# Depthwise 3x3 convolution split over three engines: GpSimd takes the last addition, VectorE gets a fifth tap for the first image, transposes move between the halves of a convolution

## The reference

```python
x = x + conv_block(_ln_c(x))      # x: (32, 128, 32, 32)
# conv_block(v): avg and max of each image and channel -> 9 taps per (image, channel) by softmax;
#   depthwise 3x3 of v with these taps, + bias, + v
t = tokens(x)                     # 32 * 1024 tokens of 128 channels
t = t + moe(_ln_t(t))             # gate to 8 experts, top 2, softmax of the 2;
                                  # per expert gelu(t @ W1 + b1) @ W2 + b2, H = 512
```

## Time and profile before

| | |
|---|---|
| median of 3 runs (lowest, highest) | 1531.86 us (1531.59, 1535.68) |
| the profiled execution | 1534.89 us, span 1532.4 us |
| busy share of the span: TensorE / VectorE / ScalarE / GpSimd | 95% / 85% / 72% / 63% |
| steps of phase A | about 31 us each |

### The profile page before, as it was taken

How to read it: one execution, slowest core, us unless ns; L and a number is a source line. 1 busy time by engine, 2 the same in 40 slices (tenths; PEclk the granted TensorE clock), 3 DMA queues, 4 the chain that set the end, 5 groups by cost and what they waited for, 6 DMA issues and landing times.

```text
span 1532.4 us, 45755 instructions
## 1 busy us (share of the span) xinstructions
PE 1453.9 (95%) x12204; PEld 1114.6 (73%) x12205; DVE 1308.8 (85%) x2676; ACT 1096.7 (72%) x2514; POOL 961.6 (63%) x1069
## 2 busy tenths in 40 slices
PE   5999999999999867999999999999999999999996
PEld 2345454555545433999999999999999999999995
DVE  2468888888888984999999999999989999999995
ACT  5477777878777523777777777777777777777773
POOL 2004455545555674777777777777777777777773
PEclk8899999999999955999999999999999999999998
DMA  4211212121222127111111232223232322222222
GB/s 141 74 38 57 70 63 81 63 75 58 77 69 64 40 71 151 41 47 40 44 43 57 66 93 86 92 86 93 85 94 83 92 86 91 84 86 78 78 75 109
DMA packets 85647, 115.77 MB, mean 76 GB/s; under 512 B 17613, under 2 KB 69865, under 8 KB 85590
## 3 DMA queue, kind: packets, MB, share of 16 engines
q1 hardware_dynamic: 64886, 76.83, 17.0%
q0 software_dynamic: 18112, 34.27, 7.0%
q10 hardware_dynamic: 2592, 4.00, 0.9%
HBM read 60.08 MB, written 58.48 MB: 77 GB/s over the span
## 4 chain that ended last, share of the span: by engine, by line
POOL 38%; PE 24%; issue 23%; DVE 6%; ACT 4%; DMA 2%; POOLq 2%; SPq 1%; ACTq 0%; DVEq 0%
PE psV L902 14%; POOL token_out L542 14%; POOL xn L530 14%; POOL yt L537 9%; PE psA L840 4%; PE psV L849 3%; DVE x L1235 2%; POOL rows_by_pair L512 1%; ACT cv L628 1%; PE psT L884 1%; ACT diag L618 1%; PE psG L886 1%; DMA stage<-in_L_ffn_W_dram 1%; ACT lnv L601 1%; POOLq L542 1%
## 5 line engine op out<-in xcount | busy, mean ns | idle before, releaser
L1495 DVE TENSOR_TENSOR gl<-g,gh 128x512 f16<-128x512 f32 x620 | 489.1, 828 | 71.1 <-ACT gh L777 61.2
L512 POOL DMA_INDIRECT rows_by_pair<-rows,idx x256 | 263.6, 1030 | 318.7 <-issue 196.1
L542 POOL DMA_INDIRECT token_out<-yt,rt x310 | 338.7, 1093 | 184.7 <-POOL yt L537 133.6
L902 PE MATMUL psV<-lp,diag 128*128 128x512 f32 x576 | 274.4, 613 | 20.5 <-ACT cv L628 20.5
L777 ACT ACTIVATE gh<-g 128x512 f16<-128x512 f32 x465 | 274.5, 624 | 16.8
L770 ACT ACTIVATE g<-psT 128x512 f32<-128x512 f32 x310 | 182.2, 597 | 101.3 <-PE psT L1057 74.4
L770 ACT ACTIVATE g<-psV 128x512 f32<-128x512 f32 x310 | 184.8, 597 | 90.1 <-PE psV L1057 62.0
L530 POOL TENSOR_SCALAR xn<-rt 128x128 f32<-128x128 f32 x310 | 221.5, 721 | 14.0 <-DMA rt<-rows_by_pair 10.1
L1078 PE MATMUL psR<-wall,gh 128*128 x1240 | 221.3, 273 | 0.4 <-DVE ya L1512 0.4
L1078 PE MATMUL psG<-wall,gh 128*128 x1240 | 221.3, 273 | 0.0
L902 PEld LDWEIGHTS psV<-lp,diag 128*128 128x128 f32 x576 | 106.2, 193 | 150.9 <-issue 108.2
(11 more groups left out here) (231 smaller groups left out, 2950.2 us busy)
## 6 DMA issues: line engine op xcount, KB each, us to landing
rt<-rows_by_pair SPq DMA_DIRECT2D x155, 133.0 KB, 2.1
xb<-in_x_dram SPq DMA_DIRECT2D x32, 512.0 KB, 3.5
yq<-token_out SPq DMA_DIRECT2D x112, 128.0 KB, 2.4
out_dram<-oq SPq DMA_DIRECT2D x112, 128.0 KB
token_out<-yt,rt POOLq DMA_INDIRECT x310, 2.3
rows_by_pair<-rows,idx POOLq DMA_INDIRECT x256, 2.4
stage<-in_L_ffn_W_dram SPq DMA_DIRECT2D x1, 2048.0 KB, 8.3
ye<-token_out SPq DMA_DIRECT2D x4, 512.0 KB, 4.3
```

Source lines behind the costliest of these rows:

```text
L512: gp.indirect_dma_start(rows_dram, bass.IndirectOffsetOnAxis(ap=idx[p][:, b:b + 1].bitcast(U32), axis=0), rows[p][:, b, :], None).then_inc ...
L542: gp.indirect_dma_start(y_dram, bass.IndirectOffsetOnAxis(ap=rt[r][:, b, ID:ID + 1].bitcast(U32), axis=0), yt[r][:, b, :], None, bounds_ch ...
L902: ins = te.matmul(psConv.rearrange("p (h w) -> p h w", w=WW), diag[k][:, m, :], lp[j][:, y:y + HH // 2, dx:dx + WW], start=(m == 0), stop= ...
L1495: v.tensor_tensor(gl[side][q][:, cols], g[side][:, cols], gh[side][q][:, cols], ALU.subtract).then_inc(lo_done, 1)
```

## The change

Each image now has four taps on TensorE and five on VectorE. VectorE's first tap reads `xb` as its second operand instead of `x1`, so there is no `add_image`: the taps no longer wait for `cv`. In the loop, GpSimd adds `cv` to `x1` once VectorE's last tap is there (`taps_added`) and both halves of `cv` are (`cv_ready`); that sets `x1_ready`. In the steps written out at the end VectorE does this addition itself. GpSimd's scatter of a pair is split by image, eight indirect DMAs each, with an addition ahead of each group of eight; the second group goes out in the following step. `take` waits for `x1_ready` of the previous pair instead of `x_used`. In TensorE's queue the last two of the eight blocks of `turn` for k = 0 move from ahead of the convolution to between its halves, and both of the first two matmuls of the first half stand ahead of `variance` (k, 1), where one stood.

```diff
-    taps_pe = (PE_TAPS + (MORE,), PE_TAPS)
-    taps_dve = ([k for k in DVE_TAPS if k != MORE], DVE_TAPS)
+    taps_pe = (PE_TAPS, PE_TAPS)
+    TURN_0 = 6
...
+            def add_conv(st_, stage, k):                      # GpSimd
+                j = 2 * st_.slot(stage) + k
+                pool.wait_ge(taps_added, st_.count(stage, 2, k + 1))
+                pool.wait_ge(cv_ready, st_.count(stage, 4, 2 * k + 2))
+                gp.tensor_tensor(x1[j][:, :], x1[j][:, :], cv[k][:, :], ALU.add).then_inc(x1_ready, 1)
...
+            def step(st_):                                    # GpSimd
+                if st_.on(3):
+                    add_conv(st_, 3, 1)
+                if st_.on(5):
+                    scatter(st_, 5, 1)
+                if st_.on(2):
+                    add_conv(st_, 2, 0)
+                if st_.on(4):
+                    scatter(st_, 4, 0)
...
-                        turn(st_, k, 0, TURN_1)               # TensorE
+                        turn(st_, k, 0, TURN_1 if k else TURN_0)
...
-                        conv(st_, k, 0, 0)
+                        for m in range(2):
+                            conv(st_, k, 0, m)
...
-                        for m in range(1, len(taps_pe[k])):
+                        for m in range(2, len(taps_pe[k])):
                             conv(st_, k, 0, m)
+                    if k == 0 and st_.on(3):
+                        turn(st_, k, TURN_0, NBLK)
...
-                                                 in1=img(x1[j]), op0=ALU.mult, op1=ALU.add)
+                                                 in1=img(xb[j] if m == 0 else x1[j]), op0=ALU.mult, op1=ALU.add)
...
                 if st_.on(3):                                 # VectorE's step
-                    window(st_, 3, 1, 0, 4)
+                    window(st_, 3, 1, 1, 4)
...
-                    add_image(st_, 0)
-                    window(st_, 2, 0, 0, 3)
+                    window(st_, 2, 0, 0, 4)
...
+                if st_.on(2):
+                    window(st_, 2, 0, 4, N_DVE)
                 if st_.on(4):
                     number(st_)
                     weigh(st_)
-                if st_.on(2):
-                    window(st_, 2, 0, 3, N_DVE - 1)
                 if st_.on(3):
                     shifts(st_)
+                if st_.on(2):
+                    window(st_, 2, 1, 0, 1)
                 if st_.on(1):
                     tap_softmax(st_)
-                if st_.on(2):
-                    add_image(st_, 1)
```

More of the change, by code:

```diff
@@ L195, in conv_moe_block @@
             sem, ("tap_ready", "z_ready", "ez_ready", "taps_ready", "diag_ready", "conv_ready"))
-        cv_ready, x_used, x1_ready = map(sem, ("cv_ready", "x_used", "x1_ready"))
+        cv_ready, x_used, x1_ready, taps_added = map(sem, ("cv_ready", "x_used", "x1_ready", "taps_added"))
         tok_ready, stat_ready, ssq_ready, tln_ready, rstd_ready, kept = map(
@@ L500, in _ @@
             tiles = pool.alloc_register("tiles")
[L501 to L511, removed]
-                    gp.indirect_dma_start(rows_dram, bass.IndirectOffsetOnAxis(ap=idx[p][:, b:b + 1].bitcast(U32), axis=0),
-                                          rows[p][:, b, :], None).then_inc(rows_out[2 * p + b // NBLK], 16)
@@ L515, in _ @@
[L515 to L519, removed]
+            pool.reg_mov(tiles, 0)
+            def add_conv(st_, stage, k):
[3 more added lines that the diff above has]
+                gp.tensor_tensor(x1[j][:, :], x1[j][:, :], cv[k][:, :], ALU.add).then_inc(x1_ready, 1)
@@ new lines, in scatter @@
+            def scatter(st_, stage, k):
+                p = st_.row_slot(stage)
+                if k == 0:
+                    pool.reg_mov(routed, st_.count(stage, 1, 1))
+                    pool.reg_mov(images, st_.count(stage, 2, 2))
+                    pool.wait_ge(s_const, 3)
+                    pool.wait_ge(routed_ready, routed)
+                    pool.wait_ge(kept, images)
+                for b in range(k * NBLK, (k + 1) * NBLK):
+                    gp.indirect_dma_start(rows_dram, bass.IndirectOffsetOnAxis(ap=idx[p][:, b:b + 1].bitcast(U32), axis=0),
+                                          rows[p][:, b, :], None).then_inc(rows_out[2 * p + k], 16)
@@ new lines, in step @@
+            def step(st_):
[7 more added lines that the diff above has]
+                    scatter(st_, 4, 0)
+            run_steps(pool, step)
+            for s in range(NU, NU + 4):
+                st_ = Step(s // 2, s % 2)
+                scatter(st_, 5, 1)
+                if st_.on(4):
+                    scatter(st_, 4, 0)
@@ L626, in take @@
                 if not st_.fixed or 2 * st_.t + st_.r > 1:
-                    act.wait_ge(x_used, st_.count(2, 2, k - 1))
+                    act.wait_ge(x1_ready, st_.count(2, 2, k - 1))
                 sc_.activation(cv[k][:, h * HALF:(h + 1) * HALF], psConv, ACT.Identity, bias=conv_b[:, :], scale=1.0).then_inc(cv_ready, 1)
@@ L931, in step @@
                     if st_.on(3):
-                        turn(st_, k, 0, TURN_1)
+                        turn(st_, k, 0, TURN_1 if k else TURN_0)
                     if st_.on(1):
                         variance(st_, k, 0)
-                    if st_.on(3):
+                    if k == 1 and st_.on(3):
                         turn(st_, k, TURN_1, NBLK)
@@ L1177, in low_b2 @@
                 v.tensor_copy(b2_e[32:33], b2low[32:33, :].rearrange("p (e d) -> p e d", e=E)).then_inc(s_low, 1)
+            N_DVE = len(DVE_TAPS)
             sd_count = dve.alloc_register("sd_count")
             c_tap = Chain(dve, ch_tap, 7)
-            c_win = Chain(dve, ch_win, len(DVE_TAPS) - 1)
+            c_win = Chain(dve, ch_win, N_DVE - 2)
             c4 = Chain(dve, ch4, 24)
@@ L1219, in tap_softmax, with add_conv @@
                 c_tap.end()
[L1221 to L1225, removed]
             def window(st_, stage, k, first, end):
                 j, n = 2 * st_.slot(stage) + k, st_.count(stage, 2, k)
-                if first == 0:
-                    c_win.begin_at(st_.count(stage, len(taps_dve[0]) + len(taps_dve[1]) - 2, k * (len(taps_dve[0]) - 1)))
-                    dve.wait_ge(x_used, n + 1)
+                c_win.begin_at(st_.count(stage, 2 * (N_DVE - 2), k * (N_DVE - 2)))
+                c_win.n = max(first - 1, 0)
                 for m in range(first, end):
-                    dy, dx = divmod(taps_dve[k][m], 3)
+                    dy, dx = divmod(DVE_TAPS[m], 3)
+                    if m == 0:
+                        dve.wait_ge(taps_ready, st_.count(stage, 1, 1))
                     ins = v.scalar_tensor_tensor(out=img(x1[j]), in0=lp[j][:, dy:dy + HH, dx:dx + WW],
-                                                 scalar=taps[st_.slot(stage)][:, taps_dve[k][m], k:k + 1],
-                                                 in1=img(x1[j]), op0=ALU.mult, op1=ALU.add)
-                    if m < len(taps_dve[k]) - 1:
+                                                 scalar=taps[st_.slot(stage)][:, DVE_TAPS[m], k:k + 1],
+                                                 in1=img(xb[j] if m == 0 else x1[j]), op0=ALU.mult, op1=ALU.add)
+                    if m == 0:
+                        ins.then_inc(x_used, 1)
+                        dve.wait_ge(x_used, n + 1)
+                    elif m < N_DVE - 1:
                         c_win.link(ins)
                     else:
-                        ins.then_inc(x1_ready, 1)
+                        ins.then_inc(taps_added, 1)
+            def add_conv(st_, stage, k):
+                j, n = 2 * st_.slot(stage) + k, st_.count(stage, 2, k)
+                dve.wait_ge(taps_added, n + 1)
+                dve.wait_ge(cv_ready, st_.count(stage, 4, 2 * k + 2))
+                dve.wait_ge(x1_ready, n)
+                v.tensor_tensor(x1[j][:, :], x1[j][:, :], cv[k][:, :], ALU.add).then_inc(x1_ready, 1)
             gates = psG[:, 0:NB2 * G].rearrange("p (b g) -> p b g", g=G)
@@ L1403, in _ @@
             second_choice(s16)
-            window(s16, 3, 1, 0, N_DVE)
+            window(s16, 3, 1, 1, N_DVE)
+            add_conv(s16, 3, 1)
             place(s16)
@@ L1408, in _ @@
             weigh(s16)
-            add_image(s16, 0)
-            window(s16, 2, 0, 0, N_DVE - 1)
+            window(s16, 2, 0, 0, N_DVE)
+            add_conv(s16, 2, 0)
             shifts(s16)
@@ L1413, in _ @@
             second_choice(s17)
-            add_image(s16, 1)
-            window(s17, 3, 1, 0, 1)
+            window(s16, 2, 1, 0, 2)
             place(s17)
@@ L1419, in _ @@
             weigh(s17)
-            window(s17, 3, 1, 1, N_DVE)
+            window(s17, 3, 1, 2, N_DVE)
+            add_conv(s17, 3, 1)
             tiles_up_to(0, NU - 1)
```

3 lines of the change are left out of this document (removed).

## The result

The changed kernel takes 1576.43 us (median of 4 runs, 1567.67 to 1577.09) against 1531.72 before (the table's three executions and one more): ratio 1.0268, 95% interval 1.025 to 1.0285. That is slower, as forecast, but by 45 us where 26 were forecast, and outside the range of 1513 to 1572. All executions here are of the ordinary kind but one of run 10, which took 2342 us and is left out of that run's ratio.

A forecast was written before the change was run, and what follows sets the result against it. TensorE was taken to bound the 31.25 us step; VectorE would then set 29.7 + 3.8 = 33.5 us. Thirteen full steps +29.3, steps 1 and 2 -3.5, in all +26: 1558 us beside 1531.86, range 1513 to 1572.

The forecast's parts named there:

- TensorE bounds the kernel, VectorE comes next; the change makes VectorE the bound: Phase A step: TensorE sets 31.25 us, VectorE 1.4 us behind; after the change VectorE 29.7 us against TensorE 29.4.
- VectorE's floor: VectorE's step in phase A after the change, before GpSimd's additions are counted: 29.7 us.
- the 1.0 us wait for `sd`: VectorE's `norm` (1, 0) comes earlier and waits for the second half's `sd`, losing 1.0 us a step.
- a kernel with no exclusion: Rival: phase A's VectorE instructions run beside GpSimd's additions; step 29.7 us, -24 us in all, 1508 us; chance 0.20.
- The moved transposes earn nothing: Two `turn` blocks moved into TensorE's 0.86 us wait for `cv` gain about nothing at the convolution's front.
- An addition takes 2.4 us: Each of GpSimd's two 128x1024 float32 additions a step takes 2.4 us, from 2.1 to 2.85.
- While it runs, a VectorE instruction with two inputs in SBUF stands: During a GpSimd addition, VectorE instructions with two SBUF inputs stand still; full exclusion with VectorE as bound had chance 0.52.
- Where they fall: Addition for (3, 1) falls into the expert choice, loss 2.1 us; that for (2, 0) stops `idx`, loss 1.7 us.
- VectorE has nothing to absorb it, since nothing it waits for is late any more: Nothing VectorE waits for in a step is late, so the additions cost their full 3.8 us a step.
- TensorE's clock falls: Rival: TensorE idles 4 us a step, its clock drops, slowing `variance` and logits 1 us a step: +13, 1571; chance 0.08.
- the main forecast: Full exclusion with VectorE as the bound: step 29.7 + 3.8 = 33.5 us, own range 1547 to 1569 us; chance 0.52.
- First steps -3.5, tail 0: Steps 1 and 2, without expert choice, gain 3.5 us from TensorE's saving; the tail's VectorE chain changes by 0.

The follow-up runs named there:

- run 10: Kernel of run 9, with GpSimd's addition for (3, 1) taken up behind the sixth of the first scatter's eight DMAs: 1523.93 us, ratio 0.9955 to the kernel before.
- Run 1: Changed kernel with GpSimd's addition cut to 8 of 1024 columns, the rest of the sum left out: 1511.09 us, ratio 0.985 to the kernel before.
- run 7: Kernel before with only the last two blocks of `turn` (k = 0) moved between the convolution's halves: 1533.61 us, ratio 0.9996.
- run 2: Changed kernel with GpSimd's addition cut to 8 columns and a 1690-column memset behind each: 1511.22 us, ratio 0.9853 to the kernel before.
- run 4: Kernel before with two spare 1024-column GpSimd additions put into each scatter, nobody waiting for them: 1589.24 us, ratio 1.0365.
- Run 5: Changed kernel with `weights_of` moved behind the step's last `inv_std` in ScalarE's queue: 1568.0 us, ratio 1.022 to the kernel before.
- run 9: Changed kernel with only VectorE's queue reordered, each image's last tap ahead of `norm`: 1538.15 us, ratio 1.0032 to the kernel before.
- run 3: Changed kernel with VectorE doing both additions in the loop too, behind each image's last tap: 1542.07 us, ratio 1.005 to the kernel before.
- run 11: Kernel of run 10 with the addition behind the fifth DMA instead of the sixth: 1573.29 us, ratio 1.0256 to the kernel before.

## Why the prediction was right and wrong

- *TensorE bounds the kernel, VectorE comes next; the change makes VectorE the bound.* Right: `zt`'s wait for TensorE is gone. Run 1 gives VectorE's floor at 29.71 us, forecast 29.7, the 1.0 us wait for `sd` included (0.8 to 1.2 seen). The forecast for a kernel with no exclusion was 24 us below before, and run 1 is 24 us below it. The parts did not fit as well: the forecast had 1.55 us a step and measured were 1.35 (before's own steps are 31.06 us as a mean, the forecast took 31.25), and the first three steps and the tail gained more than forecast.
- *The moved transposes earn nothing.* Right (run 7).
- *An addition takes 2.4 us.* Right: 2.42 as a mean, 2.36 as the median. The mean has in it two additions of 3.3 us, each begun while a tap was running on VectorE.
- *While it runs, a VectorE instruction with two inputs in SBUF stands.* Right, and shown: with the reading taken away (runs 1 and 2) the stretching goes, with spare reads it comes into the kernel before (run 4), and instructions with one input in SBUF (`norm`, run 10) are not touched. The Trainium skill's sentence on the exclusive lock ("SBUF — State Buffer", section "SBUF: two separate sides") is borne out in this: an instruction that is caught stands until the addition has ended, as `eq` does until 352.65 us beside an addition that ends at 352.48. The Trainium skill's 4497 ns for 2048 columns ("GPSIMD Engine Reference", section "Elementwise — side-by-side cycle accounting"), halved as an estimate to 2.25 us, was 0.1 us short of the median here. The stall can be longer than the addition: `eq` began 0.29 us ahead of the addition's recorded start and stood 2.53 us beside one of 2.36, and in run 4 `sc` began 0.55 us ahead and stood 2.3 us beside one of 1.90.
- *Where they fall.* Right for both; `idx` 1.81 - 0.17 = 1.64 (forecast 1.7), `eq` 2.82 - 0.29 = 2.53 (2.7 once) in eleven of twelve steps, 2.33 as a mean of the twelve. In the remaining one, from 376.56 us on, `m1h` was caught instead and stood 2.8 us, so this addition costs 2.57 us a step where 2.1 were forecast.
- *"VectorE has nothing to absorb it, since nothing it waits for is late any more."* This step failed: the sum let a stall cost its own length, 3.8 us a step, and put VectorE's wait for TensorE at nothing. Measured, the stall of `eq` makes the end of the expert choice late. ScalarE waits for that 3.3 us, in order, ahead of the `lnv` that TensorE needs; TensorE idles 2.1 us; in ten of twelve steps its clock then falls to half; the ranks come late, and VectorE waits for them, 1.24 us a step as a mean. The forecast step was 33.5, the measured one is 34.95. Of the 1.45 us missing, 1.24 are this wait; the stalls are 0.4 us longer than forecast, and small pieces beside them add up to 0.2 us less than in run 1. The wait makes 15 us in twelve steps, and the forecast for the profiled execution was 15 us too low (1561, and 1576 measured). The rest was off as well but nearly cancels: longer stalls and before's shorter steps add some 5 us, the first three steps and the tail take 3.4 off.
- *TensorE's clock falls* was a rival at 0.08, 1 us a step and 1571 us. The clock does fall, to 0.95 from 200 to 450 us where run 1 has 1.00, and its price was about right. But it was expected on the path of `variance` and the logits, because VectorE bounds the kernel and TensorE idles. It came on the path of the ranks, behind an idle time that the stall itself had made; that the price fits is luck. The two steps at full clock, with the same stalls and no wait of `pos`, last 33.9 and 33.4 us, as the main forecast has it. The four executions of the changed kernel say the same: the one at 1567.67 us had a mean granted clock of 0.959, the three at 1576 to 1577 had 0.948 to 0.951. Run 5 takes TensorE's idle time and the fall behind it away together and takes the ratio from 1.0268 to 1.022. No run holds the clock up by itself: that the wait is the clock's is read from the steps. Why the same idle time is followed by a fall in ten of them and not in two stays open.
- *First steps -3.5, tail 0.* Measured -5.5 up to the third step's start, +1.3 for the third (2.25 forecast), and -0.5 in the tail.

## What to carry to other kernels

Before work moves to GpSimd, look at what VectorE does at that moment: in this kernel a GpSimd addition whose inputs lie in SBUF stopped the VectorE instructions with two SBUF inputs that it met, until it ended, so idle time on GpSimd is not free. Put such work beside VectorE instructions with one input in SBUF (run 10 against run 9: 14 us), or leave it on VectorE if it is shorter there (run 3). When an engine is made late, follow what waits for it in every other queue, in order: the stall came back to VectorE by way of ScalarE and TensorE. And when TensorE is left idle in the middle of a step, price the clock too, step by step: two neighbouring steps with the same stalls took 33.9 us at full clock and 36.2 with the fall, and one DMA moved behind an addition (run 11) took the ratio from 0.9955 to 1.0256, with the clock fallen in eleven of twelve steps.

## What the runs showed of the hardware

A memset of GpSimd over 1690 columns (1.51 us) left VectorE's two-input instructions alone, while an addition of 2.1 us did not; beside that memset two one-input copies of 16 columns took 0.48 and 0.42 us instead of 0.17. A float32 reduction of 448 columns on VectorE kept its 0.61 us beside an addition. GpSimd's addition with both inputs from the same 128 columns took 1.90 to 2.2 us, with two separate tiles 2.34 us or more. An accumulating DMA of 512 KB within SBUF landed 4.6 to 6.6 us after its issue. Behind an idle time of 2.1 to 2.4 us in the middle of a step, TensorE's granted clock fell to 0.50 for some us in ten of twelve steps of the changed kernel, and eight records of float32 matmuls of 512 columns then took 4.89 us instead of 3.60.
